# Rows loaded as 128-byte blocks and turned by VectorE instead of TensorE

## What is computed

```
kernel = K(log_dt, C, log_A_real, A_imag)          # 64 heads x 1024, from 64 complex modes a head
mask   = arange(1024) < length[:, None]
y      = irfft(rfft(x * mask) * rfft(kernel))[:1024] + x * mask * D
x      = x + y * mask
base   = x @ W.T                                   # 1024 x 1024
gates  = softmax over the top 2 of (x @ Wr.T + 5 * onehot(language))
x      = x + base + 2 * sum_e gates[e] * (x @ A[e].T) @ B[e].T     # 8 experts of rank 16
```

## Time and profile before

| | |
|---|---|
| median of 3 runs | 664.79 us (664.57 to 667.07) |
| the profiled execution's own time | 665.17 us |
| its span | 663.4 us |
| TensorE busy | 97% |
| VectorE, ScalarE, GpSimd busy | 74%, 70%, 5% |
| rows of x: DMAs and size | 64 of 256 KB |
| matmuls | 3663, of them 256 row transposes |

### The profile page before, as it was taken

One profiled execution on the slowest core, in us unless ns is written; L12 is line 12 of the kernel. 1 busy time (PEld: TensorE's weight loads), 2 busy tenths in 40 slices (PEclk: granted clock), 3 DMA queues, 4 the chain that ended last, 5 costly groups with the idle time before them and its releaser, 6 DMA issues.

```text
span 663.4 us, 12421 instructions
## 1 busy us (share of the span) xinstructions
PE 641.9 (97%) x3663; PEld 616.3 (93%) x3663; DVE 491.8 (74%) x1504; ACT 462.5 (70%) x977; POOL 35.1 (5%) x61
## 2 busy tenths in 40 slices
PE   4798999999999999999999999999999999999997
PEld 4697989999999999999999999999999999999997
DVE  7888687777778777777877777787777778776741
ACT  5788788586776858686686868678676867864531
POOL 2241000000000000000000000000000000000000
PEclk9798999999999999999999999999999999999999
DMA  6531313333312132322213223211333321122212
GB/s 186 151 104 32 82 39 66 72 71 71 68 36 59 50 71 71 71 71 46 57 40 71 71 71 71 59 45 39 71 71 71 71 67 39 42 66 41 41 33 63
DMA packets 24064, 43.40 MB, mean 65 GB/s; under 512 B 9928, under 2 KB 14832, under 8 KB 24048
## 3 DMA queue, kind: packets, MB, share of 16 engines
q1 hardware_dynamic: 19168, 27.37, 17.9%
q10 hardware_dynamic: 4880, 15.83, 9.6%
HBM read 26.35 MB, written 16.85 MB: 65 GB/s over the span
## 4 chain that ended last, share of the span: by engine, by line
PE 91%; ACT 4%; DVE 3%; issue 1%; DMA 0%; ACTq 0%; SPq 0%; DVEq 0%
PE pmg L1269 58%; PE pc L1208 13%; PE pmg L1256 7%; PE px L1208 5%; PE px L1201 4%; PE pmg L1250 1%; DVE state L935 1%; PE pmg L1279 1%; PE pmg L1167 1%; ACT swapped L531 1%; PE pmg L1177 1%; DVE w_lo L867 0%; DMA logs<-in_L_cond_log_A_real 0%; ACT y_hi L558 0%; ACT z_swap L480 0%
## 5 line engine op out<-in xcount | busy, mean ns | idle before, releaser
L1269 PE MATMUL pmg<-w_hi,y_hi 128*128 128x384 f32 (+1 forms) x768 | 265.7, 346 | 0.7 <-DVE y_lo L982 0.7
L1269 PE MATMUL pmg<-w_hi,y_lo 128*128 128x384 f32 (+1 forms) x768 | 259.8, 338 | 0.0
L1269 PE MATMUL pmg<-w_lo,y_hi 128*128 128x384 f32 (+1 forms) x768 | 259.7, 338 | 0.0
L1269 PEld LDWEIGHTS pmg<-w_hi,y_hi 128*128 128x128 f32 x768 | 144.3, 188 | 1.7 <-issue 1.1
L1269 PEld LDWEIGHTS pmg<-w_hi,y_lo 128*128 128x128 f32 x768 | 144.4, 188 | 0.5
L1269 PEld LDWEIGHTS pmg<-w_lo,y_hi 128*128 128x128 f32 x768 | 144.3, 188 | 0.0
L531 ACT ACTIVATE swapped<-state 64x128 f32<-64x128 f32 x192 | 59.4, 309 | 65.4 <-DVE state L935 64.0
L935 DVE SCALAR_TENSOR_TENSOR state<-swapped,scan_tab,state 128x192 f32<-128x192 f32 (+1 forms) x240 | 73.8, 349 | 15.6 <-ACT swapped L531 11.1
L576 ACT ACTIVATE result<-pmg 128x384 f32<-128x384 f32 (+1 forms) x96 | 41.7, 448 | 39.4 <-PE pmg L1256 37.1
L964 DVE TENSOR_TENSOR s_lo<-state,s_hi 128x896 fp32r<-128x896 f32 x31 | 33.9, 1093 | 30.0 <-ACT s_hi L553 30.0
L982 DVE TENSOR_TENSOR y_lo<-xt,y_hi 128x1024 fp32r<-128x1024 f32 x32 | 39.2, 1225 | 20.6 <-ACT y_hi L558 19.2
(11 more groups left out here) (206 smaller groups left out, 1112.0 us busy)
## 6 DMA issues: line engine op xcount, KB each, us to landing
rows<-in_x SPq DMA_DIRECT2D x64, 256.0 KB, 5.3
out<-result ACTq DMA_DIRECT2D x60, 256.0 KB, 4.0
toe<-kpad SPq DMA_DIRECT2D x30, 128.0 KB, 5.1
rows<-in_L_cond_W SPq DMA_DIRECT2D x3, 512.0 KB, 6.9
result<-in_L_cond_W SPq DMA_DIRECT2D x3, 512.0 KB, 5.9
w_rows<-in_L_cond_W SPq DMA_DIRECT2D x2, 512.0 KB, 4.5
result<-in_L_cond_A SPq DMA_DIRECT2D x1, 512.0 KB, 6.2
b_rows<-in_L_cond_B SPq DMA_DIRECT2D x2, 256.0 KB, 6.7
```

The lines of the kernel that those rows point to most:

```text
L1269: ins = nc.tensor.matmul(pm[:, n, 0:o1 - o0], y[s][:, c, :], w[:, c, o0:o1], start=(c == 0 and y is y_hi and w is w_hi), stop=(c == CH - 1 ...
```

## The change

From pair 4 on, the rows are loaded in another shape and turned by another engine. A pair's 128x1024 values are seen as squares of 32 rows x 32 samples. `load_blocks` issues 8 DMAs a pair, for each quarter k of a chunk's 128 samples and each half d of the 64 sequences: 32 sequences x 16 (2 heads x 8 chunks) runs of 32 samples, 128 bytes each, to 32 partitions. So each square already lies in the partitions of its samples. `turn_rows` is now VectorE's: two transposes of 32x32 squares, 128x512 values each, from `rows[s]` straight to `xt[s]`. Pairs 0 to 3 are turned by TensorE as before.

ScalarE no longer copies `px` to `xt`; `split_turned` makes `u_hi` from `xt`. TensorE's transposes leave the loop and `control` takes over their waits. On VectorE, the turning of pair i+3 stands at the end of the step, behind the scan; `s_lo` moves from the end of the step to behind the next `route`; `gt_lo` moves ahead of the angles, and in even steps `zo_lo` moves from ahead of `route` to behind `gt_lo`. On SP the rows of pair i+4 wait for the turning of pair i+2 by VectorE.

```diff
--- before.py
+++ after.py
@@ -35,6 +35,7 @@
 KPITCH = 2 * P
 DUO = 4
 DUOS = HEADS // DUO
+SQUARE, HALF = 32, LEN // 2
 MAGIC = 1.5 * 2.0 ** 23
 LN2_HI, LN2_LO = 0.693359375, -2.12194440054690583e-4
 TWO_PI = 6.283185
@@ -235,6 +236,8 @@
 
         LOOPS = PAIRS // 2 - 2
         START = 16
+        TURNED_BY_PE = 64
+        BLOCK_LOADS = 16 * 8
         ROUTER = 9
         SCAN = 8
         SWAPS = 3
@@ -255,6 +258,18 @@
                     sp.dma_start(rows[s][h * SEQS:(h + 1) * SEQS, :],
                                  bass.AP(x.tensor, (2 * i + h) * LEN, [[HEADS * LEN, SEQS], [1, LEN]])
                                  ).then_inc(rows_in[s], 16)
+
+            def load_blocks(b, m):
+
+                i, s = 2 * b + m, m % 2
+                for k in range(P // SQUARE):
+                    for d in range(SEQS // SQUARE):
+                        sp.dma_start(
+                            rows[s][k * SQUARE:(k + 1) * SQUARE, d * HALF:(d + 1) * HALF].rearrange(
+                                "p (n l) -> p n l", l=SQUARE),
+                            bass.AP(x.tensor, 2 * i * LEN + k * SQUARE + d * (SQUARE * HEADS * LEN),
+                                    [[HEADS * LEN, SQUARE], [P, 2 * CH], [1, SQUARE]])
+                        ).then_inc(rows_in[s], 16)
 
             def load_w(n):
                 sp.dma_start(w_rows[n], W[n * P:(n + 1) * P, :]).then_inc(w_in[n], 16)
@@ -332,7 +347,7 @@
             store_kernel(0, 2)
             load_toe(0, 2)
             sp.wait_ge(px_full, 3)
-            load_rows(0, 4)
+            load_blocks(0, 4)
             sp.wait_ge(pm_free, 6)
             for h in range(2):
                 sp.dma_start(bass.AP(out.tensor, h * LEN, [[HEADS * LEN, SEQS], [1, LEN]]),
@@ -342,12 +357,14 @@
 
             def step(b, m, rows_left=True):
                 if rows_left:
-                    sp.wait_ge(px_full, 2 * b + m + 3)
-                    load_rows(b, m + 4)
+                    sp.wait_ge(xt_ready, 2 * b + m + 3)
+                    load_blocks(b, m + 4)
                 store_kernel(b, m + 3)
                 load_toe(b, m + 3)
 
-            step(0, 1)
+            sp.wait_ge(px_full, 4)
+            load_blocks(0, 5)
+            step(0, 1, rows_left=False)
             with sp.Fori(1, LOOPS) as b:
                 for m in range(2):
                     step(b, m)
@@ -506,6 +523,13 @@
                 if not first:
                     act.wait_ge(conv_done, i - 1)
                 nc.scalar.activation(u_hi[s][:, :, :], px[:, :, :], ACT.Copy).then_inc(uhi_ready, 1)
+
+            def split_turned(b, m):
+
+                i, s = 2 * b + m, m % 2
+                act.wait_ge(xt_ready, i + 1)
+                act.wait_ge(conv_done, i - 1)
+                nc.scalar.activation(u_hi[s][:, :, :], xt[s][:, :, :], ACT.Copy).then_inc(uhi_ready, 1)
 
             def split_toe(b, m, back=toe_back, first=False):
                 i, s = 2 * b + m, m % 2
@@ -690,7 +714,7 @@
                     split_obs(b, m + 2)
                 evacuate(b, m - 1, 2)
                 if rows_left:
-                    split_rows(b, m + 2)
+                    split_turned(b, m + 2)
                 ratios(b, m)
                 if kernels and m == 0:
                     act.wait_ge(gen_staged, b)
@@ -875,6 +899,17 @@
                 dve.wait_ge(uhi_ready, i + 1)
                 vec.tensor_tensor(u_lo[s][:, :, :], source[:, :, :], u_hi[s][:, :, :].bitcast(F32), ALU.subtract
                                   ).then_inc(ulo_ready, 1)
+
+            def turn_rows(b, m):
+
+                i, s = 2 * b + m, m % 2
+                dve.wait_ge(rows_in[s], TURNED_BY_PE + BLOCK_LOADS * (b + m // 2 - 1))
+                dve.wait_ge(ylo_ready, i - 1)
+                for d in range(SEQS // SQUARE):
+                    turned = xt[s][:, :, :].rearrange("p c (h d b) -> p h c d b", h=2, b=SQUARE)[:, :, :, d, :]
+                    blocks = rows[s][:, d * HALF:(d + 1) * HALF].rearrange("p (h c l) -> p h c l", h=2, l=SQUARE)
+                    ins = vec.transpose(turned, blocks)
+                ins.then_inc(xt_ready, 1)
 
             def split_toe(b, m, back=toe_back):
                 dve.wait_ge(thi_ready, 2 * b + m + 1)
@@ -1102,21 +1137,25 @@
             split_y(0, 2)
             for _ in scanning:
                 pass
-            split_states(0, 3)
-
-            def step(b, m, rows_left=True, kernels=True):
+            turn_rows(0, 4)
+
+            def step(b, m, rows_left=True, kernels=True, ahead=True):
                 split_toe(b, m + 1)
                 if rows_left:
                     split_ctr(b, m + 2)
-                    split_obs(b, m + 2)
+                    if m == 1:
+                        split_obs(b, m + 2)
                 if kernels and m == 1:
                     powers(b + 2)
                 route(b, m)
+                split_states(b, m + 1)
                 if rows_left:
                     split_rows(b, m + 2)
+                split_gated(b, m)
+                if rows_left and m == 0:
+                    split_obs(b, m + 2)
                 if kernels and m == 0:
                     angles(b + 2)
-                split_gated(b, m)
                 merge(b, m + 1)
                 if kernels and m == 1:
                     rotate_powers(b + 2, True)
@@ -1125,14 +1164,15 @@
                     dve.wait_ge(scan_staged, b + m // 2 + 1)
                     for _ in scan_states(b, m + 2):
                         pass
-                    split_states(b, m + 2)
+                if ahead:
+                    turn_rows(b, m + 3)
 
             with dve.Fori(1, LOOPS) as b:
                 for m in range(2):
                     step(b, m)
             step(LOOPS, 0, kernels=False)
-            step(LOOPS, 1, kernels=False)
-            step(LOOPS + 1, 0, rows_left=False, kernels=False)
+            step(LOOPS, 1, kernels=False, ahead=False)
+            step(LOOPS + 1, 0, rows_left=False, kernels=False, ahead=False)
             route(LOOPS + 1, 1)
             split_gated(LOOPS + 1, 1)
 
@@ -1231,8 +1271,12 @@
                                 (s_hi[:, h, :, :], s_lo[:, h, :, :]), False, True)
                 ins.then_inc(conv_done, 1)
 
-            def control(b, m):
-                i, s = 2 * b + m, m % 2
+            def control(b, m, alone=False):
+                i, s = 2 * b + m, m % 2
+                if alone:
+
+                    pe.wait_ge(v_copied, i)
+                    pe.wait_ge(scan, SCAN * (i - 1) + 1)
                 pe.wait_ge(uhi_ready, i + 1)
                 pe.wait_ge(ulo_ready, i + 1)
                 pe.wait_ge(chi_ready, i + 1)
@@ -1362,9 +1406,8 @@
             control(0, 3)
             project(0, 1, 2, 4, 8)
             add_lora(BANK_ORDER[2])
-            turn_rows(0, 4)
-
-            def step(b, m, rows_left=True, ahead=True):
+
+            def step(b, m, rows_left=True):
                 if rows_left:
                     turn_powers(b, m + 2)
                 wait_y(b, m)
@@ -1374,19 +1417,16 @@
                 convolve(b, m + 1)
                 add_loras(b, m)
                 if rows_left:
-                    control(b, m + 2)
-                project(b, m, 2, 0, 7)
-                if ahead:
-                    turn_rows(b, m + 3)
-                project(b, m, 2, 7, 8)
+                    control(b, m + 2, alone=True)
+                project(b, m, 2)
                 add_lora(BANK_ORDER[2])
 
             with pe.Fori(1, LOOPS) as b:
                 for m in range(2):
                     step(b, m)
             step(LOOPS, 0)
-            step(LOOPS, 1, ahead=False)
-            step(LOOPS + 1, 0, rows_left=False, ahead=False)
+            step(LOOPS, 1)
+            step(LOOPS + 1, 0, rows_left=False)
             wait_y(LOOPS + 1, 1)
             project(LOOPS + 1, 1, 0)
             project(LOOPS + 1, 1, 1)
```

## The result

The changed kernel takes a median of **645.29 us** (4 runs, 644.37 to 646.18) against 665.93 us (4 runs) of the kernel before: a ratio of 0.969, 95% interval 0.9667 to 0.9712. Forecast were 645 us and a range of 639 to 658. The profiled execution took 645.27 us, 19.9 less than the 665.17 of the one before; 20.3 were forecast.

What follows compares the result with a forecast made beforehand. TensorE, 97% busy, bounds the kernel; after the change VectorE's chain does, by a little. 13 passes x 1.43 = 18.6 plus 1.7 outside the loop body give 20.3 us off 665.17: forecast 645 us, range 639 to 658.

Steps and rivals of the forecast that it cites:

- t_lo behind the scan: VectorE, each step: t_lo starts 1.36 us after the scan ends, held by ScalarE's t_hi; 0.67 us earlier than before.
- wait for the ratio: Even step, between t_lo and gated: VectorE waits for ScalarE's exp of the ratio, 0.16 us before, 0.31 after.
- gated to merge: End of gated to merge: 3.73 us in even steps by VectorE's own work, 3.33 in odd steps by TensorE's way.
- two steps: One even plus one odd loop step, 18.36 + 18.68 = 37.04 us by VectorE's chain, against 38.47 before.
- loads: Rows in 4096 packets of 128 bytes a pair: hidden, no cost; rival of too many packets 166 us slower, chance 0.07.
- TensorE's term: Row transposes leave TensorE for pairs 4 to 31: 28 x 0.87 = 24.4 us, alone giving 36.73 per two steps.
- The sum outside the steady passes: Transposes outside the loop body, pair 4 ahead and pair 31 behind: 2 x 0.87 = 1.7 us, beside 13 x 1.43.
- The nearest row: VectorE's 128x516 operation on angle, 0.69 us, next 0.61 behind, taken for the unmeasured transposes: 1.30 us for two.
- The rival of half speed: VectorE's two transposes take 2.44 us a pair, two steps 39.20, ending at 673 us; chance 0.12.
- The point of no gain: Cost of VectorE's transposes from which the change stops paying: 2.07 us a pair.
- The move of s_lo: s_lo behind the route, ready 1.01 us behind gated; TensorE needs it at 1.84, so nobody waits for it.
- zo_lo's move: Even step: zo_lo's 0.39 us leaves the stretch from t_lo to gated and joins that from gated to merge.

## Why the prediction was right

| step of the prediction | forecast | measured |
|---|---|---|
| a transpose of 128x512 f32, start to start | 0.61 | 0.61 (0.69 alone) |
| t_lo behind the scan | 1.36 | 1.36 |
| scan to gated, even and odd | 4.97, 5.69 | 5.01, 302.95+0.29-297.56 = 5.68 |
| wait for the ratio | 0.31 | 0.34 |
| gated to merge, even and odd | 3.73, 3.33 | 3.71, 306.56-303.24 = 3.32 |
| merge to scan, from the even step | 9.66 | 297.56-287.86 = 9.70 |
| two steps | 37.04 | 37.04 |
| TensorE alone | 36.73 with its old wait | 36.53 without it |
| loads | nothing | nothing (37.05 with rows of 4 KB) |

- **The mechanism** is the one forecast: VectorE's chain once round, not TensorE's work, sets two steps. One transpose less changes nothing, three and four cost, and a shorter chain gives the time back up to TensorE's own 36.53.
- **TensorE's term** was right in size, and right in that not all of it arrives. 28 x 0.87 = 24.4 us left TensorE; with the old wait for `gated` gone too it would be 27. VectorE's chain takes 7 of them: 0.52 us per two steps, not the 0.31 of the prediction, which kept the old wait in TensorE's 36.73.
- **The sum outside the steady passes** was less exact than the total suggests. Thirteen passes were counted at 1.43 us; twelve gave it, the first only 0.80. The set of transposes behind the loop was worth the 0.87 forecast (0.90). The one ahead of it can't be read: 1.15 us are gone there, but two executions with the same instructions differ by 1.78. That the median (645.29) meets 645 to 0.3 us is in this part luck. The 37.04 rests on distances that each came out within 0.04 us of the forecast; that their errors cancel to the hundredth is luck too. Why the first pass saves less was not traced.
- **The nearest row** for an operation without a row gave the right figure: the 516-column operation on `angle` with 0.69. But its reason, that operations of one size last alike, is wrong: the operation on `angle` just ahead of it has 516 columns too and takes 0.42 (286.79). The choice between the two was partly luck, and harmless, since t_lo waits for t_hi either way, as the run with one transpose shows. The rival of half speed falls; the four transposes show where it would have ended, at 2.33 us the gain is nearly used up (662.7 us). Its price of 673 us was some 8 us too high: from 38.40 at 2.33 us, 2.44 us would make about 38.6 for two steps, an estimate, so about the time before. The point of no gain was put at 2.07 us. With the measured hiding it lies a little beyond 2.33, so the forecast's threshold was too low by 0.3 us or more; nothing in the sum hung on it.
- The figure of 311 ns for a 128x128 bf16 transpose (the Trainium skill, VectorE: DVE Perf Modes, The three transpose paths) does not scale to 8 such pieces: 2.5 us was the estimate, 1.30 for two f32 instructions of 512 columns the measurement. "Pipelined to sustain one element per cycle per lane" (the Trainium skill, Vector Engine (DVE) Microarchitecture Reference, 3.8) agrees: a 516-column operation with two inputs, which reorders nothing, lasts as long (0.70). The rule that sends a 128x128 transpose to TensorE (the Trainium skill, VectorE: DVE Perf Modes, Rules for kernel authors) is about a whole 128x128 transpose. Here the loads place the squares, so VectorE turns only 32x32 ones, and with TensorE as the bound the move paid 20.6 us.
- **The move of s_lo** was called free of harm. It is more: without it the rest of the change brings 9.4 us (655.9 against 665.3), and VectorE's new order alone 2.6, but the whole change 20.6. The prediction's sum had this in it (0.67 us earlier for t_lo in spite of 1.3 us of work), and the run without the move shows it.
- **zo_lo's move** was priced but not judged. The prediction carried 0.39 us ahead of the route and 0.39 behind it, without saying that ahead of the route most of it lay in the wait for the ratio. Moved back, it gives some 1.2 us in the loop.
- **The loads**: no transpose waits for a DMA, and eight loads of 64 KB each land after 3.6 us. A 128-byte packet takes 12 ns, close to the lower bound of 10 and far from the 72 that would have set the step. The doubling to 5.2 us a pair that the prediction took for transfers below 512 B does not show; the 10 ns that were to be doubled came themselves from packets of 8 bytes.

## What to carry to other kernels

Where one engine is busy all the time, work taken from it is worth what the next chain leaves: lay out the next chain once round, with starts and ends from the timeline, before the work is moved. Put the moved work where its new engine already waits: here the place of one instruction, s_lo, decided 10 of 20 us. After the change, ask again which operations on the new bound lie outside its waits; moving three of them, and one on ScalarE, brought another 7 us.

## What the runs showed of the hardware that was not expected

- Operations on VectorE that follow each other without a wait mostly overlap in the timeline, by 0.07 to 0.10 us (s_lo ends at 285.14, u_lo starts at 285.06): four transposes of 0.69 us take 2.33 us between their neighbours. Where the second one reads what the first wrote, there was a gap instead (`angle` to `angle`, 287.21 to 287.25). A bracket of 0.34 us of idle time stood for about 0.44 us that could be filled.
- TensorE, when it waits for `gated`, loses more than the wait shown: bracket 0.17 us, near convolution 0.56 us later in its step than where it didn't wait (9.29 against 8.73). The row ahead of the wait reads 302.86 and 0.34 long, while the rows before it start 0.17 to 0.18 apart, so the bracket begins about 0.17 late; and from the turning of `gated` to the convolution it is 0.24 us after a wait and 0.03 without one (284.77 to 284.80). With three transposes the bracket is 0.42 and the delay 0.80, with four 1.24 and 1.60.
- Eight loads of 512 runs each keep SP's queue 5.29 us, the two loads of 64 rows 1.19.

```profile
285.07 5.29 SPq L267 DMA_DIRECT2D rows<-in_x  x8
```
